# A receptance kept as exp(-r) and folded into the column pass's denominators, in a Trainium2 attention stage

## The reference, cut to what matters

```python
k = xs2 @ att_wk.T
v = xs2 @ att_wv.T
sr = jax.nn.sigmoid(xs2 @ att_wr.T)
v = _wkv(sp_decay[0] / T, sp_first[0] / T, k, v)      # along rows
v2 = _wkv(sp_decay[1] / T, sp_first[1] / T, k2, v2)   # along columns: k and v transposed in the image
att_out = sr * v @ att_wo.T
tok = tok + gamma1 * att_out
```

## Time and profile before

| | us |
|---|---|
| median of 3 runs | 5950.95 (5949.97 to 5953.04) |
| the profiled execution's own time | 5949.77 |
| its span | 5948.0 |
| PE busy | 4981.9 (84%) |
| DVE busy | 4253.6 (72%) |
| ACT busy | 3670.0 (62%) |
| POOL busy | 3588.9 (60%) |

### The profile page before, as it was taken

The page is one execution under the profiler, slowest core; times in us unless marked ns, Lnnn a source line. Parts: engine busy times, 40 slices in busy tenths (PEclk is TensorE's granted clock), DMA queues, the critical chain, the costliest instruction groups (busy, mean ns, idle before and its releaser), DMA issues. The chain is left out here.

```text
span 5948.0 us, 77644 instructions
## 1 busy us (share of the span) xinstructions
PE 4981.9 (84%) x23504; PEld 3940.7 (66%) x23504; DVE 4253.6 (72%) x5637; ACT 3670.0 (62%) x6950; POOL 3588.9 (60%) x2824
## 2 busy tenths in 40 slices
PE   5979999969966767767668664897999999999999
PEld 5969888857732433434434333676888888888888
DVE  4449999987749888888888985775555555555555
ACT  0016555546657887888888885565566565565655
POOL 0029888857748787786777874676444444444444
PEclk9989999989988988888889887999999999999999
DMA  6987666659940223213122121998422322322320
GB/s 171 264 205 185 174 176 180 167 145 265 260 111 11 66 55 77 59 40 85 48 64 66 44 66 52 244 263 220 99 57 54 87 57 54 89 55 54 89 54 24
DMA packets 388596, 674.50 MB, mean 113 GB/s; under 512 B 21117, under 2 KB 346702, under 8 KB 368910
## 3 DMA queue, kind: packets, MB, share of 16 engines
q1 hardware_dynamic: 334768, 514.71, 37.0%
q10 hardware_dynamic: 53522, 156.21, 7.1%
HBM read 437.00 MB, written 233.87 MB: 113 GB/s over the span
## 5 line engine op out<-in xcount | busy, mean ns | idle before, releaser
L1521 POOL TENSOR_TENSOR hidden_part<-hidden_whole,hidden_part 128x448 fp32r<-128x448 f32 x672 | 751.4, 1155 | 1023.2 <-ACT hidden_part L1486 1023.2
L655 POOL TENSOR_TENSOR omni_in_part<-omni_norm,omni_in_part 113x448 fp32r<-113x448 f32 x384 | 602.9, 1581 | 206.8 <-ACT omni_in_part L714 204.1
L1390 PE MATMUL f_out_ps<-hidden_part,ffn_wv_parts 128*128 128x448 f32 (+1 forms) x3360 | 720.7, 370 | 0.7 <-POOL hidden_part L1521 0.7
L1390 PEld LDWEIGHTS f_out_ps<-hidden_part,ffn_wv_parts 128*128 128x128 f32 (+1 forms) x3360 | 578.2, 177 | 103.5 <-POOL hidden_part L1521 35.5
L1195 POOL TENSOR_TENSOR input_times_v<-input_factor,v_all 128x448 f32<-128x448 f32 x336 | 419.7, 1249 | 362.9 <-ACT input_factor L1088 343.2
L1564 DVE TENSOR_SCALAR hidden_whole<-f_hid_ps 128x448 f32<-128x448 f32 x672 | 417.4, 622 | 250.0 <-POOL hidden_part L1521 157.4
L87 PE MATMUL dw_ps<-dw_in_part,dw_band_part 112*112 112x432 f32 (+3 forms) x1344 | 484.5, 361 | 77.9 <-POOL dw_in_part L474 41.3
L87 PE MATMUL omni_ps<-omni_in_part,omni_band_part 113*112 113x448 f32 x1152 | 439.7, 382 | 118.7 <-POOL omni_in_part L655 87.9
L1017 PE MATMUL proj_ps<-mixT_low,kvr_weights_low 128*128 128x448 f32 x672 | 354.7, 612 | 203.8 <-ACT k_all L1079 174.5
L1019 PE MATMUL proj_ps<-mixT_ends,kvr_weights_ends 128*128 128x448 f32 x1008 | 515.7, 595 | 0.0
L88 PE MATMUL dw_ps<-dw_in_part,dw_band_part 112*112 112x432 f32 (+3 forms) x1344 | 483.2, 360 | 0.0
(11 more groups left out here) (179 smaller groups left out, 13544.7 us busy)
## 6 DMA issues: line engine op xcount, KB each, us to landing
xin<-x SPq DMA_DIRECT2D x16, 2352.0 KB, 13.2
x_pointwise<-xp ACTq DMA_DIRECT2D x16, 2352.0 KB, 18.8
dw_in<-x_pointwise SPq DMA_DIRECT2D x24, 1568.0 KB, 24.4
y_gelu<-dw_out ACTq DMA_DIRECT2D x24, 1568.0 KB, 13.2
omni_in<-y_gelu SPq DMA_DIRECT2D x24, 1568.0 KB, 22.7
att_mix<-omni_out ACTq DMA_DIRECT2D x24, 1568.0 KB, 13.3
residual_pairs<-y_gelu SPq DMA_DIRECT2D x16, 2352.0 KB, 11.7
tok<-residual_pairs SPq DMA_DIRECT2D x16, 2352.0 KB, 9.0
```

Of the source, the lines that this page charges most:

```text
L655: pool.tensor_tensor(rounded(inner(p[1])), z[u][:, :, cc, :], inner(p[0]), ALU.subtract).then_inc(in_split, 1)
L1390: return pe.matmul(bank, rounded(w), rounded(x), start=start, stop=stop)
L1521: pool.tensor_tensor(rounded(kk[n % 2][1][:, h, :]), whole[h % KW][:, :], kk[n % 2][0][:, h, :], ALU.subtract).then_inc(kl_ready, 1)
```

## The change

The r chunks leave PSUM as exp(-r) instead of r: ACT's evacuation is Exp with scale -1 for r, Copy for k and v. `receptance` (the sigmoid over the tile and the line that names the table set) and `gate` are gone, with their semaphores. Since sigmoid(r) = 1 / (1 + exp(-r)), the column pass multiplies its denominator by (1 + exp(-r)) before the inversion. For that, in a column unit, DVE now does the numerator first, keeps the last state, waits for that copy, adds the bonus to Q in place in PSUM, waits for this, and writes (exp(-r) + 1) x Q over e, with exp(-r) read by columns. Row units are as before. POOL's last product of a column unit is written into r_all in place of v_all, and PE waits for it directly. The k evacuation of a new step waits for the last weighing of the tile two steps back.

```diff
             def evacuate(step, t, o):
                 if t == 0 and o == 0:
-                    need(act, g_done, step - 1)
+                    if step > 1:
+                        act.wait_ge(ev_done, unit_of[step - 2, False, NQ - 1].count())
                 e = entry["project", step, t, o]
                 act.wait_ge(bank_ready, e + 1)
                 to = (kS[:, step % 2, :], vS[:, step % 2, :], rS[:, step % 4, :])[o]
-                act.activation(to[:, TC * t:TC * (t + 1)], bank(e)[:, 0:TC], ACT.Copy).then_inc(bank_read, 1)
-
-            def receptance(step):
-                act.wait_ge(bank_read, entry["project", step, NCH - 1, 2] + 1)
-                act.activation(rS[:, step % 4, :], rS[:, step % 4, :], ACT.Sigmoid).then_inc(sr_done, 1)
-                act.preload_act_table_set("natural_log_exp_and_others")
+                how = (ACT.Exp, -1.0) if o == 2 else (ACT.Copy, 1.0)
+                act.activation(to[:, TC * t:TC * (t + 1)], bank(e)[:, 0:TC], how[0], scale=how[1]
+                               ).then_inc(bank_read, 1)
...
-                    if rows and unit.position == UNITS - 3:
-                        receptance(step)
...
-                pool.tensor_tensor(part_of(vS, unit), grid(EV[unit.slot % 2]), grid(E[unit.slot]), ALU.mult
-                                   ).then_inc(wkv_done, 1)
+                to = part_of(vS, unit) if unit.rows else part_of(rS, unit)
+                pool.tensor_tensor(to, grid(EV[unit.slot % 2]), grid(E[unit.slot]), ALU.mult).then_inc(wkv_done, 1)
...
+            def numerator(unit):
+                ev = EV[unit.slot % 2][:, :]
+                dve.wait_ge(p_done, unit.count())
+                dve.scalar_tensor_tensor(ev, ev, unit.bonus, P, ALU.mult, ALU.add).then_inc(n_done, 1)
...
             def outputs(unit):
+                e = E[unit.slot]
                 dve.wait_ge(q_done, unit.count())
+                if unit.rows:
+                    dve.scalar_tensor_tensor(e[:, :], e[:, :], unit.bonus, Q, ALU.mult, ALU.add).then_inc(d_done, 1)
+                    numerator(unit)
+                    keep_last(unit)
+                    return
+
+                numerator(unit)
+                keep_last(unit)
+                dve.wait_ge(kept, unit.count())
+                dve.scalar_tensor_tensor(Q, e[:, :], unit.bonus, Q, ALU.mult, ALU.add).then_inc(bonus_done, 1)
+                dve.wait_ge(bonus_done, unit.tile * NQ + unit.q + 1)
+                dve.wait_ge(bank_read, entry["project", unit.tile, NCH - 1, 2] + 1)
+                dve.scalar_tensor_tensor(grid(e), part_of(rS, unit), 1.0, Q.rearrange("p (a b) -> p a b", b=W),
+                                         ALU.add, ALU.mult).then_inc(d_done, 1)
-
-            def gate(tile):
-                r = rS[:, tile % 4, :]
-                dve.wait_ge(sr_done, tile + 1)
-                dve.wait_ge(wkv_done, unit_of[tile, False, NQ - 1].count())
-                dve.tensor_tensor(r, vS[:, tile % 2, :], r, ALU.mult).then_inc(g_done, 1)
```

More of the change, by code:

```diff
@@ L831, in attention @@
         kt_done = m.sem("k_by_column_done")
-        sr_done = m.sem("receptance_ready")
-        g_done = m.sem("wkv_gated")
+        bonus_done = m.sem("column_denominator_done")
         out_ps_ready = m.sem("attention_out_in_psum")
@@ L939, in part_of @@
         def part_of(t, unit):
+            slot = unit.tile % t.shape[1]
             if unit.rows:
-                return t[:, unit.tile % 2, unit.q * QT:(unit.q + 1) * QT].rearrange("p (a b) -> p a b", b=W)
-            by_column = t[:, unit.tile % 2, :].rearrange("p (r w) -> p w r", r=W)
+                return t[:, slot, unit.q * QT:(unit.q + 1) * QT].rearrange("p (a b) -> p a b", b=W)
+            by_column = t[:, slot, :].rearrange("p (r w) -> p w r", r=W)
             return by_column[:, unit.q * QW:(unit.q + 1) * QW, :]
@@ L1025, in project_out @@
                 if group == 0:
-                    pe.wait_ge(g_done, 3 * pair + 2 + n)
+                    pe.wait_ge(wkv_done, unit_of[3 * pair + 1 + n, False, NQ - 1].count())
                 for jp in (2 * group, 2 * group + 1):
@@ L1255, in sums, with keep_last @@
                 scan(unit, 1, P, EV[unit.slot % 2]).then_inc(p_done, 1)
+            def numerator(unit):
+                ev = EV[unit.slot % 2][:, :]
+                dve.wait_ge(p_done, unit.count())
+                dve.scalar_tensor_tensor(ev, ev, unit.bonus, P, ALU.mult, ALU.add).then_inc(n_done, 1)
+            def keep_last(unit):
+                dve.tensor_copy(last[unit.slot][:, :], PQ[:, :, QT - 1]).then_inc(kept, 1)
             def outputs(unit):
-                e, ev = E[unit.slot][:, :], EV[unit.slot % 2][:, :]
+                e = E[unit.slot]
                 dve.wait_ge(q_done, unit.count())
[L1260 to L1265, removed]
-            def gate(tile):
-                r = rS[:, tile % 4, :]
-                dve.wait_ge(sr_done, tile + 1)
-                dve.wait_ge(wkv_done, unit_of[tile, False, NQ - 1].count())
-                dve.tensor_tensor(r, vS[:, tile % 2, :], r, ALU.mult).then_inc(g_done, 1)
+                if unit.rows:
[11 more added lines that the diff above has]
+                                         ALU.add, ALU.mult).then_inc(d_done, 1)
             def add_residual(image, group):
@@ L1287, in _ @@
                 for unit in steps[step]:
-                    if unit.position == 1 and step > 1:
-                        gate(step - 2)
                     sums(unit)
@@ L1298, in _ @@
             add_residual(B - 2, NCH - 1)
-            gate(TILES - 1)
             for group in range(NCH):
```

## The result

The changed kernel takes 6649.5 us (median of 4 runs, 6643.8 to 6651.0) against 5950.9 before: a ratio of 1.117, 95% interval 1.115 to 1.119. The forecast was 6578, with a range of 6440 to 6720. The profiled execution took 6643.8 us, its span is 6642.0.

The account below looks back on a forecast made before the run. In the attention stage DVE led with ACT 100 us behind; table loads would make ACT the bound. 5949.8 + 615 for the window + 12 for the last step = 6577, shown as 6578 us; range 6440 to 6720.

Parts of the forecast that it names:

- The decisive step: Attention stage, ACT: without the preload every unit pays two table loads, 2.72 us, 875.8 us for the window's 322 units.
- ACT's sum: Attention window, steps 1 to 23: ACT's work 2262 us plus idle time 193, window 2455 us, which is +615.
- The last step: From 3600 to 3652 us: seven more units' loads, 19 us, about 7 in ACT's idle time, +12 us.
- Covered, and its cost is 0: DVE in the attention window: 1653 us of work, at most 1728, in 2455, so its added column work costs nothing.
- first rival: Attention stage: one table set serves all, no loads left in the loop; 5817 us, 5892 with slow stride; chance 0.04.
- Order and latency: Column units: denominator ready 2.1 us behind the P scan instead of 0.6; no new wait, without loads about 1.1 us.
- One set for all: The first rival: compiler gives the run a set with Exp and Ln, 5817 to 5892 us, chance 0.04.
- Loads that hide: Attention stage: loads partly run while Ln's operand is awaited; ACT idle 51 to 80 us, 6436 to 6465, chance 0.1.
- TensorE at the lower level: Attention projections: pauses start each k, v, r group at 1.2 GHz; idle 263 + 256 us, time 6904, chance 0.12.

Follow-up runs that it names:

- experiment 1: Changed kernel plus one line naming the table set natural_log_exp_and_others once, ahead of the attention stage's step loop: 5890.5 us, 0.990 of the kernel before.
- experiment 2: Kernel before with only its line that names the table set taken out; sigmoid and gate stay: 6789.6 us, ratio 1.141.
- experiment 3: Changed kernel with the table set named once, ahead of step 12, so that 161 of 336 units pay loads: 6251.4 us.
- experiment 6: Column denominators' factor read from a contiguous constant tile instead of r by columns: 5842.8 us with the table set named once, 6643.7 us in the changed kernel.
- experiment 7: Changed kernel with the set named once and DVE's column order changed, bonus sum first and over e in SBUF: 5845.7 us, ratio 0.982.
- experiment 5: Changed kernel with idle matmuls ahead of r projections: 40 ahead of 68 of 168, 6876.2 us; then 24 or 48 ahead of 32, 6644.0 us.
- ACT's half: Kernel before with the set named once ahead of the loop and the sigmoid left out, gate and column units kept: 5822.0 us, ratio 0.978.
- DVE's half: Gate replaced by seven products a tile, going from the 5822.0 us of ACT's half to the 5890.5 us of experiment 1: costs 68 us.

## Why the prediction was right

**The decisive step** (every unit pays two loads once no set is named) was right in count and price: 672 loads were forecast at Ln and Exp, 672 are there, and the stretch that priced them measures 3.75 us again. Experiments 1, 2 and 3 show it as the cause from three sides.

**ACT's sum.** Work was put at 2262 us and is 2204. The loads' duration alone, 643 by 1.283, is 825 us, and 1509.0 - 129.2 + 825 = 2205 is all there is. The 50 us on top of it, for the overlap that a load takes from its neighbours, don't appear in ACT's busy time; where they went is not shown. Nor do the 6 us for r's Exp: it takes 543 ns where the Copy took 541; the 577 ns of the sum were those of the inverting Exp, which reads another tile. Idle time was put at 193 and is 316 us. The term that was mis-sized is r's wait: 68.3 + 46 = 114 forecast, 202.6 measured. The mean clock was forecast well (0.77; 0.78 measured); the error was to spread the lower level evenly over the projections, which gave 29 slow ones more for r (18% of 161). In the whole stage the slow projections (over 2.5 us) went from 12 to 81 of 168 for r, but only from 35 to 36 for k and from 9 to 12 for v: the long pauses of the changed kernel stand ahead of r. k kept 24.2 us that I had let go, v 38.1 instead of 25.5. With 58 us less work and 3 us less of short gaps that is +65 for the window (2520 against 2455), of the 67 us between 6577 and the profiled execution's 6643.8.

**The last step** was put at +12 and is +14.

**DVE.** "Covered, and its cost is 0" was right (experiment 6), but the cost itself was too low. In experiment 1 a column unit takes 3.67 us from the start of its P scan to the next unit's carry and a row unit 2.27, 1.40 more where 0.80 was forecast: the stride adds 0.37, and the numerator, which had always had another instruction between itself and the P scan, waits 0.19 us for it. It would have mattered in the first rival, forecast at 5817 to 5892: experiment 1, which is that case, gave 5890.5, at its upper end, and partly by luck: DVE's work was put at 1728 us and its waits at 54, and they are 1705 and 75.

**Order and latency.** No wait of ACT for the later denominator appears under the loads, as forecast. Without loads it does, as forecast too: 82.8 us of the Ln's waiting in experiment 1.

**The rivals.** One set for all: the right mechanism, and not what the program does unless a line asks for it. Loads that hide: ACT's idle time was 316 us and not under 80. TensorE at the lower level: it came in part, as 88 us of r waits beyond the forecast, and not as 250 or more.

## What to carry to other kernels

A line that names or warms a state (here a table set) serves everything that runs until the next change of state, not only the code that it stands in. Before it is deleted with that code, count in the trace what happens in the stretch where it hasn't yet run. Here ten loads in the first 50 us of a stage foretold 672. A gain on one engine can also be paid for on the one that leads: ACT's half was worth 115 us, DVE's half took 68 back.

## What the runs showed of the hardware that was not expected

- A scalar_tensor_tensor of 128 x 448 that reads one operand from SBUF at 224 bytes of stride takes 994 ns on DVE, 620 contiguous.
- DVE waits about 0.19 us for its own scan when nothing stands between (2519.48 - 2518.25 = 1.23 us from the P scan to the numerator in the changed kernel, against 1.04 in its row units, 2510.97 - 2509.93), and 0.12 us for a short copy or 0.15 us for a sum (0.19 and 0.72 us from start to start, against 0.07 and 0.57 between neighbours that don't wait).
- A DVE product with both tensors in SBUF lengthens POOL's instruction beside it: single ones to 2.2 us where the longest had been 1.39, and all 93 over 1.4 us beside such a product (experiment 7).
- 77 of 81 slow r projections of the changed kernel came after 4.2 to 24.6 us without a matmul; with those pauses filled, 11 of 68 were slow instead of 53 (experiment 5). After bursts that left a pause of 2.23 us most were slow and one was not, so that the pause's length alone doesn't settle it.
